# Eight experts of a small mixture: inputs gated before, or outputs gated after, in a kernel around a recurrence

## The reference

```python
h = jax.nn.relu(jnp.einsum('tm,emh->eth', cont, W1) + b1[:, None, :])   # 64 -> 512, 8 experts
y = jnp.einsum('eth,ehm->etm', h, W2) + b2[:, None, :]                  # 512 -> 64
expert_out = jnp.einsum('etm,te->tm', y, gate)
```

## Time and profile before

| | |
|---|---|
| time, median of 3 runs | 5803.53 us (5802.18 to 5803.68) |
| profiled execution: span from the first to the last instruction | 5801.0 us |
| mean granted TensorE clock | 0.996 of full speed |
| TensorE busy | 5580.6 us |
| VectorE busy | 5403.5 us |
| GpSimd busy | 5287.9 us |
| ScalarE busy | 4595.4 us |

### The profile page before, as it was taken

One profiled execution on the slowest core, in us unless ns is written; L12 is line 12 of the kernel. 1 busy time (PEld: TensorE's weight loads), 2 busy tenths in 40 slices (PEclk: granted clock), 3 DMA queues, 4 the chain that ended last, 5 costly groups with the idle time before them and its releaser, 6 DMA issues.

```text
span 5801.0 us, 88242 instructions
## 1 busy us (share of the span) xinstructions
PE 5580.6 (96%) x28770; PEld 3073.1 (53%) x28770; DVE 5403.5 (93%) x9108; ACT 4595.4 (79%) x9941; POOL 5287.9 (91%) x2828
## 2 busy tenths in 40 slices
PE   6999999999999999999999999999999999999998
PEld 3555555555555555555555555555555555555554
DVE  5999999999999999999999999999999999999997
ACT  5878878788788787887887878878878788788786
POOL 5999999999999999999999999999999999999997
PEclk9999999999999999999999999999999999999999
DMA  6454544544444445444454454444444444444443
GB/s 166 113 121 107 122 115 111 123 112 116 120 108 121 116 111 122 112 116 120 108 120 117 110 121 113 115 120 109 119 118 110 120 114 114 120 110 118 119 109 88
DMA packets 158222, 673.41 MB, mean 116 GB/s; under 512 B 45761, under 2 KB 46785, under 8 KB 92225
## 3 DMA queue, kind: packets, MB, share of 16 engines
q1 hardware_dynamic: 157762, 667.76, 48.0%
HBM read 617.26 MB, written 50.33 MB: 115 GB/s over the span
## 4 chain that ended last, share of the span: by engine, by line
PE 76%; ACT 14%; DVE 7%; issue 3%; SPq 1%; DMA 0%; POOL 0%; ACTq 0%; POOLq 0%
PE bank L973 17%; PE bank L921 15%; PE ps_y L887 11%; PE ps_acc L985 9%; PE bank L1037 8%; PE ps_acc L1037 8%; ACT h L598 4%; PE bank L908 4%; DVE ps_z L1144 4%; ACT conte L707 3%; DVE ps_z L1138 2%; ACT wide L718 1%; PE bank L1020 1%; PE ps_acc L1020 1%; PE bank L959 1%
## 5 line engine op out<-in xcount | busy, mean ns | idle before, releaser
L525 POOL TENSOR_TENSOR u<-xb,bt 128x1024 f32<-128x1024 f32 x2048 | 4811.0, 2360 | 387.1 <-DVE ps_z L1144 315.6
L598 ACT ACTIVATE h<-ps_z 128x512 f32<-128x512 f32 x4096 | 2408.0, 599 | 1008.3 <-DVE ps_z L1144 807.9
L1138 DVE TENSOR_TENSOR ps_z<-h,ps_A 128x512 f32<-128x512 f32 x4096 | 2664.7, 691 | 314.7 <-ACT h L598 233.1
L1144 DVE TENSOR_TENSOR ps_z<-ps_z,u 128x512 f32<-128x512 f32 x4096 | 2655.3, 691 | 0.0
L973 PE MATMUL bank<-wide,w 65*128 65x256 f32 x4096 | 1015.0, 393 | 18.5 <-ACT wide L718 18.5
L887 PE MATMUL ps_y<-h,c_wide 128*32 128x512 f32 x8192 | 962.0, 599 | 49.0 <-ACT h L598 49.0
L921 PE MATMUL bank<-xnT,w_enc 128*128 128x256 f32 x4096 | 901.3, 381 | 2.8 <-ACT wide L671 2.8
L973 PEld LDWEIGHTS bank<-wide,w 65*128 65x128 f32 x4096 | 730.6, 189 | 315.3 <-issue 152.6
L921 PEld LDWEIGHTS bank<-xnT,w_enc 128*128 128x128 f32 x4096 | 772.9, 190 | 158.9 <-issue 53.3
L887 PEld LDWEIGHTS ps_y<-h,c_wide 128*32 128x32 f32 x8192 | 227.2, 109 | 566.8 <-issue 418.1
L908 PE MATMUL bank<-w_in,xnT 128*128 128x512 f32 x1024 | 474.4, 606 | 7.6 <-DVE c_wide L1214 1.6
(11 more groups left out here) (124 smaller groups left out, 4285.1 us busy)
## 6 DMA issues: line engine op xcount, KB each, us to landing
xb<-x_proj_scratch SPq DMA_DIRECT2D x2048, 256.0 KB, 4.6
xbuf<-in_L_attn_x SPq DMA_DIRECT2D x256, 128.0 KB
xres<-in_L_attn_x SPq DMA_DIRECT2D x512, 64.0 KB
out<-g SPq DMA_DIRECT2D x256, 128.0 KB
x_proj_scratch<-xp SPq DMA_DIRECT2D x256, 64.0 KB
w_in<-in_L_attn_w_in SPq DMA_DIRECT2D x1, 2048.0 KB, 8.1
w_enc<-in_L_ffn_W_enc SPq DMA_DIRECT2D x1, 2048.0 KB, 16.5
w_dec<-in_L_ffn_W_dec SPq DMA_DIRECT2D x1, 2048.0 KB, 20.4
```

Source lines behind the costliest of these rows:

```text
L525: pool.tensor_tensor(u[:, tau % 2, :, :], xt, bt[:, :, :], ALU.mult).then_inc(u_ready, 1)
L598: act.activation(h[:, tau % RING, f, :], ps_z[:, f, :], ACT.Tanh).then_inc(h_ready, 1)
L1138: dve.tensor_tensor(ps_z[:, f, :], h[:, (tau - 1) % RING, f, :], ps_A[:, f, :], ALU.mult).then_inc(m_done, 1)
L1144: dve.tensor_tensor(ps_z[:, f, :], ps_z[:, f, :], u[:, tau % 2, f, :], ALU.add).then_inc(z_ready, 1)
```

## The change

- The inputs of the experts are no longer gated. `contT` (64 rows) is doubled by two matmuls onto both row halves (`dup`, `dup_copy` into `contT_both`). `scale_cont`, `conteT_transpose`, `conteT_copy`, `gateT_transpose`, `gateT_copy` and the bias matmul go.
- W1 lies as four pairs of experts, one on rows 0 to 63, the other on 64 to 127. Eight rounds: `up` does four matmuls of 64 rows, 128 hidden units and 256 tokens, alternating between the row halves, each half with its own bank. `relu` is two activations of 256 columns a bank with the bias as a per-partition operand. `down` does four matmuls, the two experts on the two column halves.
- ps_acc holds the results of a pair side by side, two pairs at a time. `g_spread` spreads the gates over 64 rows each by 16 matmuls of 128 tokens with a broadcast weight, ScalarE copies them out (`g_copy`), and VectorE does `(result + b2) * gate` four times a block on 128x256 (`gate_pair`). `fold` adds the pairs and halves with eight matmuls.
- `fin_y` goes, and `fin_gate` moves from GpSimd to VectorE, reading y in PSUM.
- b1 and b2 are loaded as rows ahead of the first step and turned by a matmul.
- All slots are new, and the fills of the banks are counted from the order of the slots.

```diff
-            def scale_cont(blk, q):
...
-                act.activation(conte[:, q, :, M], gate[:, q, :], ACT.Copy)
-                for e in range(E):
-                    ins = act.activation(conte[:, q, e, 0:M], cont_acc[:, q, :], ACT.Copy,
-                                         scale=gate[:, q, e:e + 1])
...
+            def dup(blk):
...
+                for j in range(2):
+                    ins = pe.matmul(bank[0][M * j:M * j + M, 0:T2], halves, contT[:, :], start=True, stop=True)
+            def g_spread(blk, n):
...
+                for i in range(2):
                     for q in range(2):
+                        c0 = T2 * i + P * q
+                        for j in range(2):
+                            e = 2 * (2 * n + i) + j
+                            ins = pe.matmul(bank[n][M * j:M * j + M, c0:c0 + P],
+                                            gate[:, q, e:e + 1].to_broadcast([P, M]), ident[:, :],
+                                            start=(i == 0 and q == 0), stop=True, skip_group_check=True)
+            def up(blk, r):
...
+                for j in range(2):
+                    wait_free(pe, f"UP{r}{j}", blk)
+                for c in range(2):
+                    t = 2 * (r % 2) + c
+                    for j in range(2):
+                        rows = slice(M * j, M * j + M)
+                        ins = pe.matmul(bank[j][:, T2 * c:T2 * c + T2], w_1[rows, r // 2, P * t:P * t + P],
+                                        contT_both[rows, :], start=(c == 0), stop=True, skip_group_check=True)
+                        if c == 1:
+                            filled(ins, f"UP{r}{j}")
+            def down(blk, r):
...
+                if r == ROUNDS // 2:
+                    pe.wait_ge(pair_gated, PAIRS * blk + 2)
...
+                for c in range(2):
+                    for j in range(2):
+                        t = EH // P * (2 * i + j) + 2 * (r % 2) + c
+                        ins = pe.matmul(pair_acc[M * j:M * j + M, i % 2, :], w_2[:, t, :], hidden[:, r % 2, j, c, :],
+                                        start=(r % 4 == 0 and c == 0), stop=(r % 2 == 1 and c == 1),
+                                        skip_group_check=True)
+            def fold(blk):
...
+                for i in range(PAIRS):
+                    for j in range(2):
+                        ins = pe.matmul(eo_acc[M * j:M * j + M, :], halves, gated[:, i, :],
+                                        start=(i == 0), stop=(i == PAIRS - 1))
             def relu(blk, n):
...
+                for c in range(2):
+                    t = EH // P * e + 2 * (r % 2) + c
+                    ins = act.activation(hidden[:, r % 2, j, c, :], bank[j][:, T2 * c:T2 * c + T2],
+                                         ACT.Relu, bias=b_1[:, t:t + 1])
+            def gate_pair(blk, i):
...
+                dve.scalar_tensor_tensor(out=gated[:, i, :], in0=pair_acc[:, i % 2, :], scalar=b_2[:, i:i + 1],
+                                         in1=spread[:, i, :], op0=ALU.add, op1=ALU.mult).then_inc(pair_gated, 1)
+            def fin_gate(blk, par):
...
+                dve.tensor_tensor(o[:, :], ps_y[:, :], gt[:, par, :], ALU.mult).then_inc(o_ready, 1)
```

The slots that the prediction speaks of:

```diff
+SP_CHUNK = (-5.75, 2.1875, 4.125, 4.6875, 5.25, 16.25, 19.1875, 21.5625)
+SP_STORE_SCRATCH = -26.875
+ACT_G_COPY = (14.75, 14.5)
+ACT_RELU = (9.5, 10.9375, 12.875, 12.9375, 13.5, 13.875, 15.6875, 15.9375, 16.5, 16.9375, 17.5625, 17.6875, 18.6875, 18.75, 20.5, 20.625)
+ACT_DEC_SQUARE = (28.625, 31.125)
+PE_Y = (17.8125, 21, 23.625, 29.625, 30.8125, 33.0625, 40.3125, 41.5)
+PE_G = (24.75, 24.375)
+PE_UP = (20.75, 23.25, 23.375, 25.625, 26.3125, 27, 27.6875, 29.8125)
+PE_DOWN = (23.1875, 24.75, 25.625, 26.625, 27.1875, 29.625, 30.75, 31.625)
+DVE_ROUTE = (8.9375, 9.75, 10.1875, 10.375, 10.9375, 11.5625)
+DVE_DEC_SCALE = (31.9375, 33.8125)
+DVE_DEC_SHIFT = (32.875, 34.875)
+DVE_FIN_MUL = 41.375
+DVE_GATED = (17.75, 18.125, 22.5, 23.1875)
+DVE_FIN_GATE = 35.875
```

More of the change, by code:

```diff
@@ L42 @@
 M = 64
-MA = M + 1
 E = 8
+PAIRS = E // 2
+ROUNDS = E
 EH = 512
 T2 = 2 * P
-NFILL = 34
 LN_EPS = 1e-5
@@ new lines, in build, with wait_filled, wait_drained @@
+        bank_of = {name: side for side in range(2) for name, _ in FILLS[side]}
+        filled_as = {}
+        for side in range(2):
+            order = sorted((STEPS * blk + slot, blk, k) for k, (_, slot) in enumerate(FILLS[side]) for blk in range(NB))
+            for n, (_, blk, k) in enumerate(order):
+                filled_as[FILLS[side][k][0], blk] = n + 1
+        def wait_filled(eng, name, blk):
+            eng.wait_ge(bank_filled[bank_of[name]], filled_as[name, blk])
+        def wait_drained(eng, name, blk):
+            eng.wait_ge(bank_drained[bank_of[name]], filled_as[name, blk])
@@ L941, in router @@
                     tokens = contT[:, P * q:P * q + P]
-                    ins = pe.matmul(routed[:, q, :], tokens, w_r[:, :], start=False, stop=True,
+                    ins = pe.matmul(routed[:, q, :], tokens, w_r[:, 0:E * E], start=False, stop=True,
                                     skip_group_check=True)
                 ins.then_inc(logits_ready, 1)
-            def gateT_transpose(blk):
-                pe.wait_ge(conte_ready, 2 * blk + 2)
-                for q in range(2):
-                    ins = pe.transpose(gateT_acc[:, P * q:P * q + P], gate[:, q, :], ident[:, :])
-                ins.then_inc(gateT_ready, 1)
@@ L1102, in between @@
                     router(blk)
-                for n in range(4):
-                    if slot == PE_CONTET[n]:
-                        conteT_transpose(blk, n)
-                if slot == PE_GATET:
-                    gateT_transpose(blk)
-                for n in range(9):
-                    if slot == PE_EXPERTS[n]:
-                        experts(blk, n)
-                if slot == PE_EO_FOLD:
-                    eo_fold(blk)
+                if slot == PE_DUP:
+                    dup(blk)
+                for n in range(2):
+                    if slot == PE_G[n]:
+                        g_spread(blk, n)
+                for r in range(ROUNDS):
+                    if slot == PE_UP[r]:
+                        up(blk, r)
+                for r in range(ROUNDS):
+                    if slot == PE_DOWN[r]:
+                        down(blk, r)
+                if slot == PE_FOLD:
+                    fold(blk)
                 for n in range(2):
@@ L1247, in between @@
                         dec_shift(blk, q)
+                for i in range(PAIRS):
+                    if slot == DVE_GATED[i]:
+                        gate_pair(blk, i)
+                if slot == DVE_FIN_GATE:
+                    fin_gate(blk, par)
                 if slot == DVE_FIN_MUL:
```

450 lines of the change are left out of this document (180 added, 270 removed).

## The result

| | before | changed |
|---|---|---|
| time, median | 5803.6 us (5802.2 to 5817.3) | 5879.4 us (5865.2 to 5884.2) |
| ratio of the two | | 1.0123, 95% interval 1.0107 to 1.0139 |
| profiled span | 5801.0 us | 5876.1 us |
| TensorE, VectorE busy | 5580.6, 5403.5 | 5325.5, 5513.0 |
| GpSimd, ScalarE busy | 5287.9, 4595.4 | 5207.9, 4507.5 |

The forecast was 5785 us. The kernel is slower than the one before by 1.2%, where it was to be faster by 0.3%. One of the prediction's own signs of being wrong came true: u waits for its chunk.

What follows compares the result with a forecast made beforehand. VectorE was taken to set the pace: floor 87.2 plus stalls 1.7 gives 88.9 us a block against 89.17, 64 x -0.27 = -17; head +1, tail -3, so 5782 of span, 5785 us; range 5755 to 5815, whole 5710 to 5900.

Steps and rivals of the forecast that it cites:

- u waits for its chunk: Sign of being wrong: GpSimd's u would wait for the load of its chunk, where u(16) was put ready by 0.2 us.
- The rule for extra VectorE work: Extra VectorE work behind a step's second add hides 0.16 us of its pitch; elsewhere it costs all of it.
- the floor of 87.2: VectorE's time for a block of 32 steps: 81.9 us undisturbed plus 5.3 of extras, 1.5 more than before.
- the final product: VectorE's final product, now between multiplies and adds, costs 1.20 us a block; TensorE reaches it within 0.1.
- The four gatings: VectorE's four gated pairs, 256 columns at 0.36 us each; three cost that, one behind the second add 0.20: 1.3 a block.
- TensorE: right in kind and size: TensorE's busy time falls by 6.2 us a block, 86.8 to 80.6, worth only the 2.7 of ring waits.
- rival C: The gate spreads don't overlap on TensorE, 1.7 to 2.2 us each instead of 1.0, stalling VectorE: 109 us, 5894; chance 0.18.
- The ring waits: Tanh's waits for TensorE to give back a slot of the ring of h, 2.7 us a block, would go.
- The stalls of the rounds: Matmul and relu handovers on single banks stall VectorE, mainly in steps 13 to 16; with smaller waits 1.7 us a block.
- The SP queue, "I take 0": The projection's store ahead of chunk 4 costs nothing: chunk 4 lands 4.6 us after issue, u(16) ready by 0.2.
- rival D: Chunk 4 comes late: 1 us more delay in the store makes u(16) late by 0.8; 51 us, 5836; chance 0.10.
- Head and tail: Two more loads and a small copy before the first step cost 1 us; the earlier-ending decoder half and dropped copy save 3.

Runs made afterwards that it cites:

- e6: The changed kernel with the projection's store behind chunk 4, plus matmuls adding zero in TensorE's waits ahead of up(2), up(4) and up(5): 5752 us.
- e1: The changed kernel with one slot moved, the store of the projection behind chunk 4 in SP's queue instead of ahead of it: 5777 us.
- e8: The changed kernel with chunk 4 left late, plus matmuls adding zero in TensorE's waits, three instead of one ahead of up(5): 5847 us.
- e5: e4 with the gate product moved behind the skip product and the gatings of pairs 2 and 3 behind the second add of step 22: 5774 us.
- e3: The changed kernel with two slots moved, the projection's store behind chunk 4 and y(2) ahead of up(2) in TensorE's list: 5772 us.
- e4: e3 with the product of y and silu(gate) as before the change, a copy by ScalarE and the product on GpSimd: 5759 us.

## Why the prediction was wrong

In the order of its steps:

- **The rule for extra VectorE work and the floor of 87.2: right but for one place.** Undisturbed steps take 2.56; the excess of steps 31, 0, 1, 2, 3 is 0.50, 0.55, 0.49, 0.43, 0.43, where 0.50, 0.44, 0.50, 0.44, 0.44 stood; the final product costs 1.22 (1.20). The four gatings, 0.24, 0.38, 0.24 and 0.38, are 1.24 (1.3). The third, between the two adds, hides its 0.16 too, which the rule denied it; that and a pitch above the one taken cancel in the sum. One of 256 columns, put at 0.36 from the earlier trace rows, has a pitch of 0.39, from the starts of the pair below (VectorE's timeline of the changed kernel). By these sums the change costs VectorE 1.5 us a block, and that part was never to be had back.

```profile
2836.05 0.47 DVE L1153 SCALAR_TENSOR_TENSOR wide<-ps_acc,bias_cols,wide 128x256 f32<-128x256 f32 x1
2836.44 0.69 DVE L1088 TENSOR_TENSOR ps_z<-h,ps_A 128x512 f32<-128x512 f32 x1
```

- **TensorE: right in kind and size.** An up group takes 1.06, both spreads together 2863.59 to 2865.39, 1.80 (2.0 was taken; rival C is out). The ring waits are gone. The gain has no taker, as the prediction said.
- **The stalls of the rounds: 1.7 forecast, 1.2 found** in e6 (88.40 - 87.2), where nothing else disturbs. Steps 14 and 16 have 0.27 and 0.32 for 0.25 and 0.23, step 15 has 0.27 for 0.59, and step 13 none for 0.21; step 19 has 0.19 where none was forecast.
- **The SP queue, "I take 0": this step failed.** It was rival D, held at one chance in ten and at 51 us. The prediction had the store's place, its length and its wait right. What it had wrong is the landing: the 4.6 us of the earlier trace rows are the median over single DMAs, and a chunk is there when the last of its four is. In the kernel before, the first to fourth DMA of a chunk land 3.3, 4.2, 4.9 and 5.6 us after their own issue (medians), and so they do, within 0.1, in the changed kernel. With 5.6 in place of 4.6 and a slack of 0.2, the sum would have had u(16) late by 0.8, rival D's case. In the block above the fourth DMA went out at 2824.06, 0.3 to 0.7 later than I had it, and landed 5.77 on, 1.2 more than 4.6; u(16) started 3.2 us into step 15 instead of 1.3 to 1.7. By the blocks without a fall that was worth 1.08 us, 69 in all; by the means of e1 and e8, 1.58 us a block or 101 us, falls of the clock that came with it included.
- **The clock: missing from the sum.** The prediction read full clock in the earlier trace rows, a trace with TensorE at 96%, and didn't ask what gaps would do to it. With TensorE at 91% it falls in 41 of 62 blocks, and the mean block is longer than one without a fall by 0.85. With the chunk on time it costs 0.40 a block (e1 against e6), 25 us; the rest comes only with the late chunk, and part of that rest is the chunk's own (step 16 stalls 2.57 in the blocks of the late falls, 1.65 in those without).
- **Head and tail: as forecast.** The first step starts at 66.19 (64.82 before, +1 forecast), but in the experiments it lies anywhere from 61.96 to 67.36, so that this match is luck. The last square comes 2.6 us after the last step's start (2.4 forecast, 4.8 before):

```profile
5848.57 1.30 DVE L1088 TENSOR_TENSOR ps_z<-h,ps_A 128x512 f32<-128x512 f32 x2
...
5851.13 0.60 ACT L709 ACTIVATE hidden<-ps_acc 128x512 f32<-128x512 f32 x1
```

Together: 88.9 forecast; -0.5 for the rounds, +0.40 for the clock, +1.58 for the chunk make 90.38, the mean block measured; the two last terms are differences of measured means, so that this is an account and no test. Without the two failures the change gives e6's 5752, faster than before by 0.9%.

What stays open: why blocks with the same list differ in whether the clock falls. In e1 the falls come 355.0 or 443.7 us apart, that is every fourth or fifth block, in e5 every third (266.2 us); what that spacing hangs on wasn't tried. Chunk 4's last DMA lands after 5.84 us behind the store and after 5.58 in e1 (medians); how much of these 0.26 is the store's isn't shown. Why it lands a microsecond later still in some blocks isn't shown either.

The Trainium skill's sentence that was weighed (TensorEngine Tiling, PSUM Bottleneck: tiling speeds TensorE, not the emptying of PSUM) agrees with the waits of steps 14 to 16: in e3 TensorE stands 1.72 us ahead of the spreads for the relus. It wasn't what turned the sign.

## What to carry to other kernels

When a change shortens the engine that isn't the pace setter, its gain is only what it stops making others wait; add up the pace setter's list with the rule of its own loop, and the floor comes out to a tenth of a microsecond a block. Then give every reordered queue the same care, the DMA queue first: a late load has no cover of its own, and one slot of it decided the sign here. A load that is split over several DMAs is there when the last one is, and the median over all of them isn't that time: 4.6 against 5.6 us here. A TensorE with new gaps may also lose its clock: where nothing else fits in, matmuls of zeros into an open accumulation cost nothing here (88.36 us a block against 88.38 for e1's blocks without a fall) and gave back 25 us.

## What the runs showed of the hardware

The granted clock falls to its lower level in stretches that begin when TensorE has waited, in the changed kernel in two thirds of the blocks (41 of 62). In 28 of them the fall comes in steps 13 and 14, around the end of 1.82 us of waiting for relus ahead of up(2) or up to 1.6 us behind it; in 13 it comes in steps 17 and 18, most often after 1.6 to 3.6 us of waiting for relus ahead of up(5) and 0.6 for the gating. One such stretch costs 1.64 us when it lies on the rounds and the chunk is in time. More work on the same engine kept the clock at its upper level. In e4's profiled run there was no fall, in e5's, with a near equal list, there were 20. The four timed runs of e4 took 5744 us at a mean clock of 0.995 and 5757 to 5764 at 0.992 to 0.993: the scatter goes with the clock. The four DMAs of a chunk land 3.3, 4.2, 4.9 and 5.6 us after their own issue (medians, kernel before), so that a chunk is complete 5.6 us after its last issue. Eight matmuls of 128 columns on alternating column halves, with a broadcast weight, take 0.90 us (half of 2863.59 to 2865.39), as side by side as the four of 256 of a down group (2865.39 to 2866.35, 0.96).
